# A decoder kernel's 16-wide attention heads: stores of q's and k's parts to the scratch, issued and waited for by halves

## The reference, cut to what matters

```python
def _L1_attn_ref(x, Wq, bq, Wk, bk, Wv, bv, Wo, bo):
    B, S, D, H = (4, 512, 256, 16)
    rx = _apply_rope(x)
    def proj(W, bias):
        y = rx @ W.T + bias
        return y.reshape(b, s, h, hd).transpose(0, 2, 1, 3)
    q, k, v = (proj(Wq, bq), proj(Wk, bk), proj(Wv, bv))
    scores = jnp.einsum('bhqd,bhkd->bhqk', q, k) / np.sqrt(hd)
    attn = jax.nn.softmax(scores, axis=-1)
    attended = jnp.einsum('bhqk,bhkd->bhqd', attn, v)
    return attended.transpose(0, 2, 1, 3).reshape(b, s, d) @ Wo.T + bo
```

## Time and profile before

| | |
|---|---|
| median of 3 runs | 2109.47 us (2102.84 to 2113.85) |
| the profiled execution's own time | 2103.16 us |
| its span, first to last instruction | 2101.8 us |
| busy share of the span | PE 80%, DVE 59%, ACT 49%, POOL 47% |
| mean granted clock of PE | 0.908 of full |
| steps of the changed stage (first to last product at L1403 and L1414) | 655.5 to 1090.6 us |

### The profile page before, as it was taken

The page is one execution under the profiler, slowest core; times in us unless marked ns, Lnnn a source line. Parts: engine busy times, 40 slices in busy tenths (PEclk is TensorE's granted clock), DMA queues, the critical chain, the costliest instruction groups (busy, mean ns, idle before and its releaser), DMA issues. The chain is left out here.

```text
span 2101.8 us, 23811 instructions
## 1 busy us (share of the span) xinstructions
PE 1683.6 (80%) x7418; PEld 1232.8 (59%) x7419; DVE 1234.1 (59%) x2317; ACT 1032.3 (49%) x1981; POOL 988.7 (47%) x824
## 2 busy tenths in 40 slices
PE   5698894999935887878882989989998998679882
PEld 2477673777723665656652656656666665556661
DVE  5655554666547685959853665575675674452224
ACT  2154442555401675757782665665675765052220
POOL 1200002243233474657770574574674676048884
PEclk9899997999965898999996999999999999669996
DMA  2300003444235222213002010120120110138776
GB/s 78 122 11 31 1 21 126 114 126 111 61 85 130 71 61 62 50 46 85 21 1 98 21 42 21 32 61 21 31 60 24 29 52 24 59 77 200 179 178 161
DMA packets 96787, 146.17 MB, mean 70 GB/s; under 512 B 22711, under 2 KB 61820, under 8 KB 93830
## 3 DMA queue, kind: packets, MB, share of 16 engines
q1 hardware_dynamic: 65104, 102.69, 16.9%
q0 software_dynamic: 18432, 26.36, 6.9%
q10 hardware_dynamic: 13126, 15.60, 2.4%
HBM read 101.83 MB, written 36.41 MB: 66 GB/s over the span
## 5 line engine op out<-in xcount | busy, mean ns | idle before, releaser
L2183 POOL TENSOR_TENSOR STp_lo_use<-ST_use,STp_hi_use 128x512 fp32r<-128x512 f32 x256 | 333.8, 1312 | 227.8 <-ACT ST_use L2032 226.7
L1712 POOL TENSOR_TENSOR STp_lo<-ST,STp_hi 128x512 fp32r<-128x512 f32 x192 | 255.8, 1349 | 141.1 <-ACT ST L1480 140.3
L2096 DVE TENSOR_REDUCE nmax_use<-bank 128x1 f32<-128x512 f32 x256 | 173.3, 679 | 114.4 <-PE bank L1940 110.0
L2028 ACT ACTIVATE STp_hi_use<-bank 128x512 fp32r<-128x512 f32 x256 | 153.0, 597 | 173.2 <-PE bank L1966 170.4
L1476 ACT ACTIVATE STp_hi<-bank 128x512 fp32r<-128x512 f32 x256 | 158.8, 620 | 82.2 <-PE bank L1414 81.5
L1601 DVE TENSOR_REDUCE nmax<-bank 128x1 f32<-128x512 f32 x256 | 168.6, 680 | 41.5 <-PE bank L1403 41.0
L1403 PE MATMUL bank<-rows_k,rows_q 65*128 65x512 f32 x256 | 125.4, 498 | 66.0 <-DVE nmax L1601 48.1
L1480 ACT ACTIVATE ST<-bank 128x512 f32<-128x512 f32 x256 | 160.0, 625 | 0.0
L2032 ACT ACTIVATE ST_use<-bank 128x512 f32<-128x512 f32 x256 | 151.8, 593 | 2.1 <-POOL STp_lo_use L2183 2.1
L1940 PE MATMUL bank<-ks,qs 128*128 128x512 f32 x256 | 112.2, 440 | 36.2 <-DVE nmax_use L2096 14.9
L918 POOL TENSOR_SCALAR veps<-mv 128x4 f32<-128x4 f32 x4 | 0.9, 228 | 249.6 <-DVE mv L867 249.6
(11 more groups left out here) (428 smaller groups left out, 4558.6 us busy)
## 6 DMA issues: line engine op xcount, KB each, us to landing
stage<-in_W SPq DMA_DIRECT2D x16, 1024.0 KB, 4.9
Wgu<-in_Wgu SPq DMA_DIRECT2D x32, 384.0 KB, 3.4
rows_q<-hop_scratch SPq DMA_DIRECT2D x32, 256.0 KB, 4.6
ks<-ks SPq DMA_DIRECT2D x64, 128.0 KB, 2.3
rinv<-rinv_scratch SPq DMA_DIRECT2D x64, 128.0 KB, 2.9
rows_k<-hop_scratch SPq DMA_DIRECT2D x24, 256.0 KB, 5.6
hop_scratch<-qkp_hi SPq DMA_DIRECT2D x20, 256.0 KB
Wda<-in_Wdn SPq DMA_DIRECT2D x32, 128.0 KB, 3.6
```

The lines of the kernel that those rows point to most:

```text
L1712: G.tensor_tensor(STp[u % NHI][1], ST[u % NFULL], plain(STp[u % NHI][0]), ALU.subtract).then_inc(low["pool"].sem, low["pool"].inc(u))
L2028: A.activation(STp[u % NHI][0], bk.ap, ACT.Exp)
L2096: V.tensor_reduce(nmax[:, (h % 2) * TB + j:(h % 2) * TB + j + 1], bk.ap, AX.X, ALU.max, negate=True).then_inc(bk.free, 1)
L2183: G.tensor_tensor(STp[u % NHI][1], ST[u % NFULL], plain(STp[u % NHI][0]), ALU.subtract).then_inc(low["pool"].sem, low["pool"].inc(u))
```

## The change

ACT's wait before a piece (n, g) of a batch above 0 is for the last store of the other tensor's half g alone, and no longer for both halves. SP's wait for a half's bank stands directly before that half's stores, and no longer before the stores of both. SP's entries are written at steps 30 and 36 in place of 33 and 39. The number of transfers, their sizes and all the arithmetic are the same.

```diff
@@ act(): high part of a piece
                         if b:
-                            all_hopped(A, b if n else b - 1, 1 - n)
+                            A.wait_ge(hopped[1 - n][g].sem, hopped[1 - n][g][b if n else b - 1, len(HOPS[1 - n]) - 1])
                         A.activation(stack_out(b, n, 0, g), bk.ap, ACT.Identity, ...).then_inc(stack_high.sem, ...)
@@ sp(): stores of the pieces
                 for n in range(2):
-                    b = of_next(s, (33, 39)[n])
+                    b = of_next(s, (30, 36)[n])
                     if b:
-                        for g in range(DC):
-                            SP.wait_ge(stack_bank(b, n, g).free, stack_bank(b, n, g).free_at["stack", b, n, g])
                         if b > 1 and n == 0:
                             for i in range(QUARTERS):
                                 SP.wait_ge(stacked[i].sem, stacked[i][b - 2, 3])
                         for g in range(DC):
+                            SP.wait_ge(stack_bank(b, n, g).free, stack_bank(b, n, g).free_at["stack", b, n, g])
                             hop(SP, b, n, g)
```

## The result

The changed kernel takes 2085.28 us, median of 6 runs (2084.51 to 2093.63), against 2107.85 us for the kernel before (6 runs, 2102.48 to 2114.02): ratio 0.9903, 95% interval 0.9884 to 0.9923, faster by 1.0%. The forecast was 2091, a gain of 18.7 us; the ratio makes it 0.0097 x 2107.85 = 20.4 us (16 to 24 by its interval), the medians 22.6. The profiled execution took 2085.25 us with a span of 2083.9, 17.9 less than before's.

What follows compares the result with a forecast made beforehand. Engines wait in a ring, none full; ACT's 12.6 us of waits for q's stores lie on its path. Waits 12.0 and clock 6.7 sum to 18.7 us: 2109.47 to 2090.8, say 2091; own range 2086 to 2096, outer 2080 to 2104.

Steps and rivals of the forecast that it cites:

- (1): SP's stores of q's half 0 no longer wait for half 1: 4.8 us earlier in batch 1, landing at 698.4.
- (2): ACT starts k's half 0 when PE's products end: 5.6, 3.3 and 3.1 us earlier in batches 1 to 3, 12.0 us.
- (3): ACT's wait before k's half 1 in batch 1: none taken, 0.9 us by one of three landing estimates.
- (4): PE's clock stays full without the stops in batches 1 to 3: 6.7 us, ends 0 and 9.
- each of the three terms behind the stops: Half clock saved behind ACT's stops: 2.0 us in batch 1, 1.6 + 0.4 in batch 2, 1.4 + 0.3 in batch 3.
- The fourth term: Batch 1, window 714.7 to 718.0: 3.3 us at half clock go away, worth about 1.0 us.
- (5): SP's stream keeps its order and the new step numbers cost nothing: 0, bounds -0.5 and +0.5 us.
- The first rival: Remaining short stops bring PE's clock down elsewhere in the same stretch: gain 12 us, 2097.5 us; chance 0.25.
- The second rival: SP is held by something else or half 0's pair lands no earlier: no gain, 2109.5 us; chance 0.09.
- the third: Slower: denser ring puts PE at half speed for many more stretches in batches 1 to 3, 2121.6 us; chance 0.04.
- Two of the signs named beforehand: Steps from 655 to 1072 in place of 1090.6; mean granted clock staying at 0.908 or falling would be wrong.

Runs made afterwards that it cites:

- the kernel with the filled stops: Kernel before, plus 20 unread products on PE behind the products of k's half 0 in batches 1 to 3; ratio 0.9978, median 2102.45 us.
- each kernel with one edit alone: Against the changed kernel, one undone: SP's four stores together (ratio 0.9924, 2089.83 us), or ACT waiting for both halves (ratio 0.9959, 2097.82 us).
- ACT's edit alone: Against the kernel before, only ACT's wait is by halves; SP still issues q's four stores together; ratio 0.9924, median 2089.83 us.

## Why the prediction was right, point by point

The mechanism is shown, and its size within 0.1 us of the terms that belong to the three places: waits 12.0 and clock 2.0 + 2.0 + 1.7 make 17.7, and the preparations lost 17.8. Of the whole time, 17.8 us would be a ratio of 0.9916, which lies inside the measured interval.

(1) The early pair: SP stood ready, and the store followed DVE by 0.03 us. The landing, which no row of before showed, was taken as 698.4 by the end of the nearest transfer; the pair takes 5.6 to 6.3 us from its first issue, where 698.4 - 691.2 meant 7.2. The lower of the two bounds, 6.1, was nearer. It changed nothing, because PE's products came later still; by the upper bound, 8.8, batch 1 would have lost 0.8 us of its gain.

(2) ACT's start: in batch 1 half 0 of k follows the first high part of q by 9.50 us, against 15.14, so 5.6 as forecast. In batches 2 and 3 it is 12.42 against 15.90 and 12.46 against 15.51. That is 3.5 and 3.1, with 3.3 and 3.1 forecast; 0.2 of the 3.5 comes from the start of that preparation, between the two high parts of q, which began at a clock of 0.50 before (797.99 to 799.00) and at 1.00 after.

(3) The wait before k's half 1 did not come, as taken.

(4) The clock: each of the three terms behind the stops is confirmed by the kernel with the filled stops. The fourth term, 1.0 us for the window of 714.7 to 718.0, is confirmed in its sign but not in its size. At the same place behind k's half 1 the clock is 1.00 in the changed kernel, and also in the one with the filled stops, which kept all three waits: 18 products fit in 3.3 us there, 10 before. But each kernel with one edit alone has 1.00 there as well, although a low clock stood just ahead of it, so it may have gone by chance. Its size is hidden in the rest: the untouched stretches changed by 1.6, 0.2 and 2.3 us, and in the profile with the same order and the old step numbers by 3.8, 0.0 and -0.3. They come to 294 in both profiles, some 4 us less than in before's, but to 297.4 with the filled stops and 291.5 with ACT's edit alone. Nor does their length follow their clock: the middle stretch is as long at 0.88 as it was at 0.94. Whether those 4 us follow from the change or from where the clock's low times happened to fall, the runs do not settle.

(5) SP's order: the old step numbers give the same order and, within the interval, the same time.

The first rival expected the short stops to bring the clock down again at these very places. It did not: PE's stops of 1.56 us are there and the clock is 1.00 over all three preparations. The Trainium skill, "TensorE: Matmul & The Clock Gate", section "A second HAM failure mode: psum-queue depth-cycling", tells of another kernel in which frequent short idle times of PE made the clock go back and forth. Here it does so in the untouched stretches (0.92 and 0.88 on average in the first two, 0.89 and 0.94 before), and not at the places of the change. The second rival is out by the waits, the third by the time.

The offset between the profiled execution and the median, 6.3 us, was kept in the forecast, and that is where 2091 missed 2085. For the profiled execution the forecast was 2084.5, and it took 2085.25. After, the profiled execution lies on the median (2085.25 and 2085.28). Before, it (2103.16) lay beside the fastest of the runs (2102.48 and 2102.84), 6.3 us under the median of three and 4.7 under that of six; the median of three was itself 1.6 too high. So the median came out at 2085.28, below the forecast's own range of 2086 to 2096 by less than 1 us and inside the range of 2080 to 2104. That the profiled execution came within 0.8 us is in part luck too, since the other stages gave back what the untouched stretches gained.

Two of the signs named beforehand were less sharp than they read. The steps ended at 1069.8, not 1072, because the untouched stretches were shorter too. And the mean granted clock, which was to rise from 0.908, reads 0.910 in the profile and 0.908 to 0.910 in the six runs, so two of them would by this sign alone have spoken against the prediction. It is an average over six stages, in which the clock fell elsewhere, as in the stretch behind batch 2's preparation (0.94 to 0.88). The clock of the preparations themselves, 0.82, 0.85 and 0.94 before and 1.00 after, is the sign that holds.

## What to carry to other kernels

When an engine waits for a transfer only so that a buffer may be overwritten, look at how many transfers that wait really covers: each half of the buffer needs its own reader gone, and the reader of the first half can start when that half is written. A stop of the matrix engine can cost more than its length. Here 12 us of stops carried 5.7 us of half clock behind them, and the size of that share can be had by filling the stops with idle products. Cut a stage at fixed instructions when the total is noisy: the three preparations measured 17.8 us where the totals said 18 to 23, and repeated within 0.3 us from profile to profile.

## What the runs showed of the hardware that was not expected

A pair of 256 KB stores that is queued with two more behind it lands as soon as a pair alone: 5.6 to 6.3 us after its first issue with the four together, 6.1 (and in batch 2 at most 5.5) with half 1 alone. Four stores of 256 KB, two of them a plain copy to a scratch of another order, land within 8.0 us; the plain copies moved at 381 GB/s in the microsecond from 697, the others at 184 to 205 GB/s where they ran alone (699 to 703 before). What makes the difference was not tried.

ACT's stops of 3.4 and 3.1 us in batch 1, with either edit alone, still left the clock low behind them: from k's half 0 to its half 1 it took 6.8 and 6.3 us, against 4.75 without a stop. The stops of 0.5 and 0.3 us in batches 2 and 3 of ACT's edit alone did not: 11.05 and 11.04 us, as in the changed kernel. Nor did a stop of ACT by itself: with the filled stops ACT waited 12.7 us in total, and the clock stayed at 1.00.
